# Four graph layers in one kernel: the seams between its phases rewritten

## The reference

```python
h = jnp.maximum(_layernorm(x, axis=-1), 0.0)
x = x + _L0_gnn_ref(h, adj, L0_gnn_Wq, ..., L0_gnn_Wo, L0_gnn_bo)   # q, k, v; adj as score bias; softmax; @ Wo
h = jnp.maximum(_layernorm(x, axis=-1), 0.0)
x = x + _L1_gnn_ref(h, adj, ...)   # 2 rounds: u = (h W h^T)/temper, exp(u)*adj, normalised, @ h_lin; layer norm, relu
h = jnp.maximum(_layernorm(x, axis=-1), 0.0)
x = x + _L2_gnn_ref(h, adj, ...)   # 2 rounds: softmax(h h^T)*adj; upper part @ hl, diagonal * hs, lower part @ hr; layer norm, relu
h = jnp.maximum(_layernorm(x, axis=-1), 0.0)
x = x + _L3_gnn_ref(h, adj, ...)   # q, k, v with biases; scores + beta*adj, masked by adj > 0; softmax; no output projection
```

## Time and profile before

| | us |
|---|---|
| Median of three timed runs | 2747.0 (2746.38 to 2747.94) |
| The profiled execution | 2743.93 |
| Its span in the trace | 2742.1 |
| PE busy | 2665.8 (97%) |
| DVE, ACT, POOL busy | 1787.8 (65%), 1250.4 (46%), 1095.4 (40%) |
| Mean granted clock of PE | 0.992 |

### The profile page before, as it was taken

How to read it: one execution, slowest core, us unless ns; L and a number is a source line. 1 busy time by engine, 2 the same in 40 slices (tenths; PEclk the granted TensorE clock), 3 DMA queues, 4 the chain that set the end, 5 groups by cost and what they waited for, 6 DMA issues and landing times. The chain is left out here.

```text
span 2742.1 us, 78262 instructions
## 1 busy us (share of the span) xinstructions
PE 2665.8 (97%) x31118; PEld 2316.4 (84%) x31118; DVE 1787.8 (65%) x4041; ACT 1250.4 (46%) x2184; POOL 1095.4 (40%) x1075
## 2 busy tenths in 40 slices
PE   6999999998999999999989999999999989999998
PEld 5888888887888888888878888888888868888887
DVE  5777777775555555555567777777777775656564
ACT  4444444444444444444443433333433435655564
POOL 2343334443322432332234444435345344455455
PEclk9999999999999999999999999999999999999999
DMA  4222212224212212211221111111111112322221
GB/s 143 74 70 65 63 60 70 73 73 145 58 35 79 82 35 59 82 49 43 72 76 50 58 50 46 56 47 50 55 41 56 55 60 71 95 73 84 88 83 61
DMA packets 187135, 183.87 MB, mean 67 GB/s; under 512 B 79616, under 2 KB 186880, under 8 KB 187008
## 3 DMA queue, kind: packets, MB, share of 16 engines
q1 hardware_dynamic: 187008, 181.99, 21.9%
HBM read 131.61 MB, written 50.33 MB: 66 GB/s over the span
## 5 line engine op out<-in xcount | busy, mean ns | idle before, releaser
L58 PE MATMUL banks<-w_hi,hT_hi 128*128 128x384 f32 x1152 | 403.3, 350 | 8.7 <-PEq L2512 7.1
L58 PE MATMUL banks<-hT_hi,w_hi 128*128 128x512 f32 (+1 forms) x954 | 370.4, 388 | 22.9 <-DVE l_qT L579 13.2
L58 PE MATMUL banks<-w_hi,hT_lo 128*128 128x384 f32 x1152 | 388.6, 337 | 0.0
L58 PE MATMUL banks<-w_lo,hT_hi 128*128 128x384 f32 x1152 | 387.9, 337 | 0.0
L58 PE MATMUL banks<-hT_hi,w_lo 128*128 128x512 f32 (+1 forms) x954 | 356.6, 374 | 0.0
L58 PE MATMUL banks<-hT_lo,w_hi 128*128 128x512 f32 (+1 forms) x954 | 355.9, 373 | 0.0
L302 POOL TENSOR_TENSOR l_s_d<-l_s_b,l_mx 128x768 f32<-128x768 f32 x128 | 188.8, 1475 | 247.8 <-DVE l_mx L604 191.5
L1290 ACT ACTIVATE l_m<-banks 128x512 f32<-128x512 f32 x192 | 114.8, 598 | 370.9 <-PE banks L58 367.0
L58 PE MATMUL banks<-w_hi,l_hT_hi 128*128 128x384 f32 x768 | 268.6, 350 | 7.6 <-DVE l_left L2132 3.4
L58 PE MATMUL banks<-w_hi,l_hT_lo 128*128 128x384 f32 x768 | 257.7, 336 | 0.0
L58 PE MATMUL banks<-w_lo,l_hT_hi 128*128 128x384 f32 x768 | 257.2, 335 | 0.0
(11 more groups left out here) (208 smaller groups left out, 6122.7 us busy)
## 6 DMA issues: line engine op xcount, KB each, us to landing
after_l<-l_xr SPq DMA_DIRECT2D x192, 192.0 KB, 1.9
l_xl<-after_l SPq DMA_DIRECT2D x37, 768.0 KB, 4.7
l_xr<-after_l SPq DMA_DIRECT2D x32, 768.0 KB, 4.5
xa<-in_x SPq DMA_DIRECT2D x16, 768.0 KB, 5.4
l_xr<-in_x SPq DMA_DIRECT2D x64, 192.0 KB, 2.4
l_xr<-after_l SPq DMA_DIRECT2D x64, 192.0 KB, 2.4
out_x<-l_xr SPq DMA_DIRECT2D x64, 192.0 KB, 2.1
xa<-after_l SPq DMA_DIRECT2D x11, 768.0 KB, 6.9
```

Source lines behind the costliest of these rows:

```text
L58: last = nc.tensor.matmul(out, lhs[a](c), rhs[b](c), start=(m == 0), stop=(m == n - 1))
```

## The change

One semaphore counts the stores of all phases (`stored`), and one buffer `xr` holds the residual rows of them all, so that SP of the next phase waits for what the last phase stored. The first x comes in two halves with a semaphore each, and statistics, roots, shifts and normalisation of group 0 go by pairs of tiles; Wq and Wk have semaphores of their own. In the last turn of l0 PE makes four products of l1 in place of two; at the end of l1 three more products of l2 and four transposes; at the end of l2 all six query and key products of l3 and two value products. ACT's `y_copy` and POOL's `result` go in the last turns, and `own_result` on DVE adds straight from PSUM (l0) or from `y_rows` (l3). l2's first biases and adj are loaded in l1, and l3's constants and adj in l2.

```diff
@@ attention_phase, SP
         if proj:
-            sp.dma_start(xl[:], rows(x_in, 0)).then_inc(xl_in, 16)
-            load_weights(sp, raw, own_weights, shared["w_loaded"])
+            first = rows(x_in, 0)
+            sp.dma_start(xl[:, 0:2, :], first[:, 0:2, :]).then_inc(xl_first, 16)
+            sp.dma_start(xl[:, 2:TILES, :], first[:, 2:TILES, :]).then_inc(xl_in, 16)
+            for s, signal in enumerate((wq_in, wk_in, shared["w_loaded"], shared["w_loaded"])):
+                sp.dma_start(raw[:, s], own_weights[s].rearrange("(c p) n -> p c n", p=P)).then_inc(signal, 16)
...
+        else:
+            sp.wait_ge(stored, stored_before)
...
-            if reload or t == TILES - 1:
+            if reload or t == TILES - 1 and not proj:
                 sp.wait_ge(stored, stores)
@@ ACT, start and last turn of l0
+                next_weight(1)
             eT_copy(i, 3)
...
-                next_weight(1)
+                next_weight(2)
             oT_parts(i, 1)
...
-                next_weight(2)
-                y_copy(i, 0)
                 normalise(i + 2, (0, 1))
...
-            normalise(0)
-            for t in range(TILES):
-                hT_parts(0, t)
-            weights(range(n_w))
+            normalise(0, (0, 1))
+            weights((0,))
+            hT_parts(0, 0)
+            hT_parts(0, 1)
+            normalise(0, (2, 3))
+            hT_parts(0, 2)
+            hT_parts(0, 3)
+            weights(range(1, n_w))
             normalise(1)
@@ DVE, last turn of l0
             row_output(i, 0)
             if ahead:
                 values(i + 1, 0)
+            else:
+                next_weight(1)
             least(i, 2)
             least(i, 3)
             statistics(i + 2)
+            if not ahead:
+                oT_parts(i, 0)
             row_output(i, 1)
...
+                for t in range(TILES):
+                    own_result(i, t)
@@ PE, last turn of l0
+            else:
+                pe.wait_ge(y_read, i * TILES - 1)
+                product_of_next(1)
             wait_apart(s_read, i * TILES + TILES)
             weigh(i, 0)
...
-                product_of_next(1)
+                pe.wait_ge(eT_set, i * TILES + TILES)
+                out_transposes(i, 0)
             wait_apart(o_set, i * 2 + 1)
             weigh(i, 1)
...
                 for t in range(TILES):
                     project(i, t)
+                product_of_next(2)
+                product_of_next(3)
@@ PE, start of l3
-            pe.wait_ge(q_set, 1)
-            queries(0, 1)
...
             pe.wait_ge(zeroed, 2)
-            wait_apart(k_set, 3)
+            pe.wait_ge(q_set, KC)
+            pe.wait_ge(v_set, 2)
+            wait_apart(k_set, KC)
             scores(0, 0)
             scores(0, 1)
-            values(0, 1)
@@ bilinear_phase, SP at the start
-        for g in range(2):
-            load_rows(0, g)
+        load_rows(0, 0)
+        sp.wait_ge(stored[1], stored_before[1])
+        load_rows(0, 1)
+        for k, name in enumerate(("L2_gnn_bl", "L2_gnn_br", "L2_gnn_bs")):
+            sp.dma_start(shared["l2_biases"][:, k], a[name][0].partition_broadcast(P)).then_inc(shared["l2_b_in"], 16)
...
@@ bilinear_phase, DVE at the start and at the end
+                dve.wait_ge(m_set, 3)
+                nc.vector.memset(psU[:], 0.0).then_inc(u_zeroed, 1)
                 weights((CARRIED, CARRIED + 1))
...
-        nc.vector.memset(psU[:], 0.0).then_inc(u_zeroed, 1)
         dve.wait_ge(consts, 80)
...
+        centred(0)
+        centred(1)
+        last_scale(0)
+        centred(2)
+        centred(3)
+        last_scale(1)
+        for x in range(TILES):
+            scaled(x)
@@ bilinear_phase, PE at the end
+        split_matmul(nc, banks[:, 4, 0:D], h_cols(0, 1), weight_of_next(RIGHT))
+        pe.wait_ge(h_set, (2 * turns + 2) * TILES)
+        for x in range(TILES):
+            nc.tensor.transpose(banks[:, 5, x * P:(x + 1) * P], xl[1][:, x, 0:P], ident[:])
+        pe.wait_ge(w_lo_set, own_set + LIN + 1)
+        for x in range(2):
+            split_matmul(nc, banks[:, 6 + x, 0:D], h_cols(0, x), weight_of_next(LIN))
@@ directed_phase, PE: first unit, and the end
+            if below is None:
+                left_part(u, 2)
+                delta_transposes(u)
+                right_part(u, 2)
+                passed(above, 1)
+                context(u, 0)
+            else:
...
         pe.wait_ge(w_lo_set, own_set + 1)
-        queries_or_keys(0)
+        queries_or_keys(0, 0)
...
+        queries_or_keys(1, 2)
+        pe.wait_ge(w_lo_set, own_set + 3)
+        pe.wait_ge(c_set, 2 * GROUPS * TILES)
+        values(0)
+        values(1)
```

More of the change, by code:

```diff
@@ L341, in projected_turn @@
             residual(i, 3)
[L342 to L345, removed]
+            if ahead:
+                result(i, 0)
         def plain_turn(i, opening, ahead, further):
@@ L379, in normalise @@
         def normalise(i, tiles=range(TILES)):
-            act.wait_ge(nbias_set, i + 1)
+            act.wait_ge(nbias_set, i + 1 + (tiles[0] // 2 if isinstance(i, int) and i == 0 else halves))
             normal = xl if isinstance(i, int) and i == GROUPS + 1 else h
@@ L640, in oT_parts, with own_result @@
             nc.vector.tensor_tensor(lo, psP[:, :, 0:D], hi.bitcast(F32), ALU.subtract).then_inc(oT_set, 1)
-        if proj:
-            statistics(0)
-            shifts(0)
-            for t in range(TILES):
-                hT_parts(0, t)
-            weights(range(2))
+        def own_result(i, t):
+            dve.wait_ge(xr_set, i * TILES + t + 1)
+            if proj:
+                dve.wait_ge(y_done, i * TILES + t + 1)
+                y = y_sums(i, t)
+            else:
+                dve.wait_ge(o_set, i * 2 + t // 2 + 1)
+                y = y_rows[:, t % 2, :]
+            nc.vector.tensor_tensor(xr[:, t, :], y, xr[:, t, :], ALU.add).then_inc(y_set, 1)
+        if proj:
+            first_sums(0)
+            first_variances(0, 1)
+            first_sums(1)
+            first_shifts(0)
+            first_variances(1, step.n)
+            first_shifts(1)
+            hT_parts(0, 0)
+            hT_parts(0, 1)
+            weights((0,))
+            hT_parts(0, 2)
+            hT_parts(0, 3)
+            weights((1,))
             statistics(1)
@@ L1108, in is_first, with m_sums @@
         return isinstance(i, int) and i == 0 and k == 0
+    def m_sums(i, k, j):
+        return banks[:, j, :] if is_first(i, k) and j < 4 else psW[j % 2]
     @block.sync
@@ L1229, in ending @@
             root(i, k, 1)
-            if k >= 2:
-                for x in range(PAIR if isinstance(i, int) and i == last and k == 3 else TILES):
+            if k >= 2 and not (isinstance(i, int) and i == last and k == 3):
+                for x in range(TILES):
                     affine(i, k, x)
@@ L1313, in unit @@
             m_part(i, k, 1)
-            if not tail:
-                weight(CARRIED)
             ended(0)
@@ L1318, in unit @@
             m_part(i, k, 2)
-            if not tail:
-                weight(CARRIED + 1)
             ended(2)
@@ L1323, in unit @@
             m_part(i, k, 3)
+            if not tail:
+                weight(CARRIED)
             m_part(i, k, 4)
+            if not tail:
+                weight(CARRIED + 1)
             m_part(i, k, 5)
@@ L1350, in _ @@
         turn(last, False)
-        for x in range(TILES):
-            norm_rows(last, 3, x)
     @block.vector
@@ L1528, in _ @@
         turn(last, False)
-        ending(last, 3)
-        for x in range(PAIR, TILES):
-            own_affine(x)
-        for x in range(PAIR):
-            result(last, 3, x)
-        for x in range(PAIR, TILES):
-            own_result(x)
+        context_statistics(last, 3, 0)
+        context_statistics(last, 3, 1)
+        dve.wait_ge(xr_in[1], turns * 16)
+        centred(0)
[6 more added lines that the diff above has]
+            scaled(x)
+        step.catch_up(step.n - 3)
+        own_result(0)
+        step.catch_up(step.n - 2)
+        own_result(1)
+        step.catch_up(step.n - 1)
+        own_result(2)
+        step.catch_up(step.n)
+        own_result(3)
     @block.tensor
@@ L2014, in unit @@
             right_copy(u, 0)
[L2015 to L2017 removed]
+            if below is not None:
                 norm_rows(below, 2)
```

324 lines of the change are left out of this document (200 added, 124 removed).

## The result

| | before | after |
|---|---|---|
| Median of 9 runs each | 2747.35 us (2744.14 to 2749.33) | 2740.14 us (2738.0 to 2742.33) |
| Ratio | | 0.9973, 95% interval 0.9963 to 0.9984 |
| Profiled execution, span | 2743.93, 2742.1 | 2740.18, 2738.4 |
| Medians of a second set of runs | 2745.82 (16 runs) | 2740.95 (11 runs), ratio 0.9982 (0.9973 to 0.9992) |

A forecast was written before the change was run, and what follows sets the result against it. PE was taken as the bound, busy 2665.8 of 2742.1 us, with only 76.3 idle to win. Terms +0.9 +4.2 -2.7 -8.5 -0.95 = -7.05 give 2736.9, or 2740.0 as a median; range 2737 to 2742.5.

The forecast's parts named there:

- P0 to P1: Seam of l0 and l1: inserted w_lo delays row_output(1), barrier 3.6 to 5.9 later, part regained behind; net +4.2 us.
- P2 to P3: Seam of l2 and l3: eight early products and earlier constants start scores 9.7 earlier, slow clock costs 1.2; net -8.5 us.
- rival 3: Second units of l1 wait for xl behind seven new loads, start gives nothing; 2742 to 2743 us, chance 0.18.
- P1 to P2: Seam of l1 and l2: earlier barrier and first unit give -6.2, contention and slow clock cost 3.5; net -2.7 us.
- The 0.5 for w_lo beside POOL: In l2's first unit, the two w_lo on DVE may run slower beside POOL's work; +0.5 us.
- The start: Start of l0: first product earlier gains 1.1, but a 4.3 us hole brings a slow stretch of 2.0; net +0.9 us.
- The end: End of l3: DVE's own_result of 0.55 replaces POOL's 0.99 for the last two rows, in a chain; -0.95 us.
- The base: Whole kernel: sum made on the profiled execution of 2743.93 us, with 3.07 added for the median of timed runs.
- Rival 1: At the new holes: no new slow stretches; without penalties and contention the sum is -16.1, time 2731 us; chance 0.13.
- Rival 2: End of l0: inserted w_lo does not delay row_output(1), or holes fill; -2.6 instead of +4.2, 2733 us, chance 0.18.
- Rival 4: Slow clock lasts through first units of l1 (+6) and l2 (+3 more); sum +2, 2749 us, chance 0.09.
- the signs named: Across the kernel: PE idle falls 4 to 14 us, l1's barrier 3 to 6 later, no DMA releasing l3's start.

The follow-up runs named there:

- e6: Changed kernel, but the last phase's biases, beta and first adj load at its own start again, its early products kept; 2744.43 us, ratio 0.9995.
- e24: Changed kernel; in l1 DVE waits for constants only ahead of the first lin_copy, and SP issues l2's seven loads behind next xl and weights; 2735.09 us.
- e7: Changed kernel, but in the last turn of l3 POOL adds the last two tiles again, not DVE; 2741.74 us, ratio 0.9981.
- e8: The kernel before, unedited, run once more for a second trace; its span was 2.7 us longer than in the first.
- e1: Changed kernel, but in l0's last turn DVE makes the second next weight's w_lo behind oT_parts(1), as before; 2738.19 us, ratio 0.9971.
- the four edits: Changed kernel with w_lo late, first q/k copies ahead of group 1's normalisation, l1's constants wait at lin_copy, l2's loads behind xl; 2729.16 us, ratio 0.9939.

## Why the prediction was right, and where not

The time was 2740.14 for a forecast of 2740.0. That it came so close is in part luck: by the traces the change gave 5.1 to 5.3 us where the sum has 7.05, and nearly all of the difference is P0 to P1.

- **P2 to P3, -8.5.** Right in mechanism and size: -8.7, -9.3, less before's own -0.3. PE's products went on to 2262.95, the barrier followed 0.3 behind, PE waited 5.26 for the value copies of ACT (forecast 5.1), and the slow stretch fell on the scores (0.50). e6 confirms that the constants had to move for it (3.6 us of it).
- **P0 to P1, +4.2.** The right sign and the right cause, and 2.5 too small (+6.7). Two terms were mis-sized. Ahead of the barrier the sum has 4.75, where P1 started 6.35 later in the first trace without the start's part (7.04 with it), above my 3.6 to 5.9, and 5.6 later in the second. The 4.75 is the middle of that range and so holds only half of the slow stretch, which came in full (0.80 over 13.9 us). Behind the barrier I had "1.25 come back" and 0.8 for the loads ahead of xl (the sum writes 0.7). In the first trace 0.5 had come back at unit 1's first product, which began 20.2 us after P1's start against 20.7 before. Then DVE waited 6.9 us for xl, which I had priced from SP's queue alone, and PE waited 1.44 for l_lin where it had waited 0.21. So the phase lost another 0.8 instead of giving back 0.55. This is rival 3's mechanism, at work inside the forecast; e24 shows its size together with the constants: 5.7 us.
- **P1 to P2, -2.7.** -2.3 by the means of two, -3.1 with all traces of this code. The two holes were 2.60 and 3.86 (forecast 2.65 and 4.1), the clock 0.71 and 0.66. The 0.5 for w_lo beside POOL did not come: the two took 2.62 together at 1427.85, while POOL had nothing (its last addition ended at 1426.80). The Trainium skill's rule ("SBUF — State Buffer", "Who interferes with whom") agrees from both sides: the w_lo of P1 at 658.24, with POOL's work under way, took 1.87.
- **The start, +0.9.** +0.3 by the means of two, +0.7 with all traces of this code. In the first trace the first product began at 15.53, not 14.8, the hole was 2.56, not 4.3, and the clock fell to 0.50 all the same. In the second they were 14.86 and 3.73. PE went on at 25.1 and 25.4, so an earlier first product only makes the hole longer.
- **The end, -0.95.** Exact as work (e7), hidden in single traces by the clock.
- **The base.** The sum was made on a profiled execution with no slow stretch in its last turn; e8 puts 3.0 us on that. Adding 3.07 for the median was the right correction. The loss that was 2.5 too small in P0 to P1 is covered by a difference of the medians that is 7.2 in one set of runs and 4.9 in the other.

Rival 1 (no new slow stretches) is out by the windows; its -16.1 should read about -15, since the sum held only half of the 2.2 that it takes off. Rival 2 (the inserted w_lo holds nothing up) is out by e1. Rival 3 had its mechanism, but not its time. Rival 4 is out: in P1's first units the clock fell once in either trace, for some 4 us, and was at 1.00 beside that, and in P2 it was back at 1.00 from 1438 us on.

Of the signs named, PE's idle sum fell by 9.4, inside the 4 to 14, and no DMA released anything in P3's start. P1's barrier came 7.0 later in the first trace, past the 3 to 6.

## What to carry to other kernels

Work made ahead of a barrier pays only where the engine would wait behind it for something that the work does not need: eight products were worth over 5 us ahead of P3 (by subtraction), where PE had waited 13.2 us for a copy behind the constants, and two were worth nothing ahead of P1 once the four edits were in, where PE, behind its first 2.2 us, waited for nothing over 0.2 us. When one engine's queue is reordered to serve an early product, count what stands behind the inserted step: a weight part that PE needed only 19 us after it was made cost 4.4 us. And at seams look at every engine's order separately: five moves of a few lines each, found from the waits of PE one at a time, gave 16.7 us (2740.95 to 2724.29), more than twice what the rewrite gave.

## What was not expected of the hardware

The granted clock at one place is not a property of the kernel. With the same code and the same waits of PE (1.72 and 0.99 us ahead of the last 96 matmuls) these took 1.60, 2.78, 2.45 and 1.60 us in four executions, two of before and two of the change. In P1 of the change the slow stretch fell at 639 us in one execution and at 654 in the other. A price for a slow stretch is an average over executions, and one profile can be off by 3 us through it alone.
